# Who adds the pairs' probabilities at the end of attention: VectorE in GpSimd's place

## The reference

```
x = x + attn(layernorm(x))       # x: [2, 2048, 512] float32
x = x + ffn(layernorm(x))        # base linear layer, and 8 low-rank experts of which 2 are chosen

q, k, v = heads(x @ Wq.T), heads(x @ Wk.T), heads(x @ Wv.T)
q, k = rope(q), rope(k)
scores = einsum('bhqd,bhkd->bhqk', q, k) / sqrt(32), masked where k > q
attn = softmax(scores, axis=-1)
ctx = einsum('bhqk,bhkd->bhqd', attn, v)     # then @ Wo.T
```

## Time and profile before

| | |
|---|---|
| time, median of 3 runs | 1654.35 us (1653.99 to 1656.61) |
| profiled execution | 1654.52 us |
| its span | 1652.8 us |
| granted clock of TensorE, mean | 0.987 |
| busy: TensorE, VectorE, ScalarE, GpSimd | 97%, 69%, 46%, 54% of the span |
| GpSimd's additions L724 | 320 instructions, 619.3 us |

### The profile page before, as it was taken

How to read it: one execution, slowest core, us unless ns; L and a number is a source line. 1 busy time by engine, 2 the same in 40 slices (tenths; PEclk the granted TensorE clock), 3 DMA queues, 4 the chain that set the end, 5 groups by cost and what they waited for, 6 DMA issues and landing times. The chain is left out here.

```text
span 1652.8 us, 25687 instructions
## 1 busy us (share of the span) xinstructions
PE 1607.6 (97%) x9536; PEld 992.2 (60%) x9536; DVE 1142.6 (69%) x2253; ACT 764.2 (46%) x1539; POOL 886.4 (54%) x559
## 2 busy tenths in 40 slices
PE   6999999899999999999999999999999987999999
PEld 4888888555555555555555555545555435777776
DVE  5666666687777777777777777767777565665664
ACT  3222222145565556556556556556655663222221
POOL 2333324346677767667667767677767792112111
PEclk9999999689999999999999999999999999999999
DMA  5554784751134125115116107107103003222321
GB/s 191 197 196 172 228 292 153 197 122 33 28 86 95 27 62 118 27 41 133 34 22 153 27 18 163 27 8 173 27 8 109 8 33 102 77 77 77 113 91 51
DMA packets 112323, 157.01 MB, mean 95 GB/s; under 512 B 11600, under 2 KB 44880, under 8 KB 112208
## 3 DMA queue, kind: packets, MB, share of 16 engines
q1 hardware_dynamic: 102368, 136.10, 29.9%
q10 hardware_dynamic: 9840, 19.40, 3.3%
HBM read 96.23 MB, written 58.72 MB: 94 GB/s over the span
## 5 line engine op out<-in xcount | busy, mean ns | idle before, releaser
L857 ACT ACTIVATE a_probs<-a_st 128x512 f32<-128x512 f32 (+2 forms) x1244 | 579.0, 537 | 414.4 <-PE a_st L774 409.6
L724 POOL TENSOR_TENSOR a_pair<-a_probs 128x1024 f32<-128x1024 f32 (+2 forms) x320 | 619.3, 1956 | 196.6 <-ACT a_probs L857 189.3
L879 DVE TENSOR_REDUCE a_part<-a_mx 128x1 f32<-128x512 f32 (+2 forms) x864 | 550.9, 680 | 167.8 <-PE a_mx L758 129.2
L758 PE MATMUL a_mx<-a_k_stack,a_q_stack 96*128 96x512 f32 (+3 forms) x768 | 286.9, 399 | 1.2 <-DVE a_part L882 0.6
L774 PE MATMUL a_st<-a_q_stack,a_k_stack 98*128 98x512 f32 (+3 forms) x732 | 255.9, 369 | 0.0
L758 PEld LDWEIGHTS a_mx<-a_k_stack,a_q_stack 96*128 96x128 f32 x768 | 139.3, 189 | 173.2 <-DVE a_part L879 78.4
L882 DVE CUSTOM_DVE_ANT_0 a_mx<-a_mx,a_mask 128x384 f32<-128x384 f32 (+1 forms) x256 | 158.7, 631 | 79.9 <-PE a_mx L758 79.9
L258 POOL TENSOR_TENSOR p_rot<-p_mul 128x1024 f32<-128x1024 f32 x32 | 90.0, 2813 | 200.9 <-DVE p_mul L489 200.9
L758 PE MATMUL a_mx<-a_k_first,a_q_stack 96*128 96x512 f32 (+3 forms) x384 | 161.9, 445 | 2.6 <-DMA a_q_stack<-qk_scratch 1.8
L774 PEld LDWEIGHTS a_st<-a_q_stack,a_k_stack 98*128 98x128 f32 x732 | 138.4, 190 | 34.6 <-ACT a_probs L857 17.0
L1122 POOL TENSOR_TENSOR f_x<-f_x,f_bias 128x512 f32<-128x512 f32 x32 | 41.5, 1330 | 213.9 <-DVE f_xn L1334 213.9
(11 more groups left out here) (171 smaller groups left out, 2017.8 us busy)
## 6 DMA issues: line engine op xcount, KB each, us to landing
a_q_stack<-qk_scratch SPq DMA_DIRECT2D x72, 256.0 KB, 4.9
a_k_stack<-qk_scratch SPq DMA_DIRECT2D x72, 256.0 KB, 8.2
qk_scratch<-p_rot_hi SPq DMA_DIRECT2D x32, 512.0 KB, 3.1
qk_scratch<-p_rot_lo SPq DMA_DIRECT2D x32, 512.0 KB, 3.9
v_scratch<-p_v_st SPq DMA_DIRECT2D x32, 256.0 KB, 6.7
ctx_scratch<-a_ctx_st SPq DMA_DIRECT2D x32, 256.0 KB, 2.4
f_ctx<-ctx_scratch SPq DMA_DIRECT2D x8, 1024.0 KB, 8.8
f_x<-in_x SPq DMA_DIRECT2D x8, 1024.0 KB, 8.1
```

The costliest lines, as they stand in the source:

```text
L724: pool.tensor_tensor(pair[:, p % 2, h:h + 2, q0:TT], probs[:, s % RING, h:h + 2, q0:TT], probs[:, (s + 1) % RING, h:h + 2, q0:TT], ALU.add ...
L758: mm = pe.matmul(bank[:, i, :], queries[t][0:96, head, qi * P:(qi + 1) * P], keys[par][c][0:96, head, 0:width], start=(i == 0), stop=not m ...
L857: act.activation(probs[:, s % RING, h, q0:TT], score_bank(g, HG * s + h)[:, q0:TT], ACT.Exp, scale=SCORE_SCALE).then_inc(exp_done, 1)
L879: dve.tensor_reduce(found, bank.rearrange("p (h n) -> p h n", n=width), AX.X, ALU.max).then_inc(max_done, 1)
```

## The change

In the last group, from pair 10 on, the additions are no longer issued by GpSimd but by VectorE, in a function `add_pair` with the same instructions, waits and semaphores. VectorE does this at the head of pair p, ahead of its split for the next stage and ahead of the transposes of a unit that ended with the pair before. Where the pair lies on the diagonal, VectorE waits for GpSimd's masking. GpSimd keeps the masking and the divisions. All other groups stay as they are.

```
+NO_ITEMS = min(p for p in range(NPAIR) if items_before(p, False) >= NITEM)
...
-        no_items = min(p for p in range(NPAIR) if items_before(p, False) >= NITEM)
-        SIX_FROM = HG * (2 * no_items + 2)
+        SIX_FROM = HG * (2 * NO_ITEMS + 2)
...
-                    pool.wait_ge(pair_done, pairs(g, p - 2))
-                    for h in range(0, HG, 2):
-                        pool.wait_ge(exp_done, exps(g, s + 1, h + 1))
-                        pool.tensor_tensor(pair[:, p % 2, h:h + 2, q0:TT], probs[:, s % RING, h:h + 2, q0:TT],
-                                           probs[:, (s + 1) % RING, h:h + 2, q0:TT], ALU.add).then_inc(pair_added, 1)
+                    if not (g == GROUPS - 1 and p >= NO_ITEMS):
+                        pool.wait_ge(pair_done, pairs(g, p - 2))
+                        for h in range(0, HG, 2):
+                            pool.wait_ge(exp_done, exps(g, s + 1, h + 1))
+                            pool.tensor_tensor(pair[:, p % 2, h:h + 2, q0:TT], probs[:, s % RING, h:h + 2, q0:TT],
+                                               probs[:, (s + 1) % RING, h:h + 2, q0:TT], ALU.add).then_inc(pair_added, 1)
...
+            def add_pair(g, p):
+
+                s = 2 * p
+                t, j = STEPS[s]
+                q0 = max(0, j + 1 - t * SUB) * P
+                if j >= t * SUB:
+                    dve.wait_ge(masked, diagonal_steps(g, s + 1))
+                dve.wait_ge(pair_done, pairs(g, p - 2))
+                for h in range(0, HG, 2):
+                    dve.wait_ge(exp_done, exps(g, s + 1, h + 1))
+                    dve.tensor_tensor(pair[:, p % 2, h:h + 2, q0:TT], probs[:, s % RING, h:h + 2, q0:TT],
+                                      probs[:, (s + 1) % RING, h:h + 2, q0:TT], ALU.add).then_inc(pair_added, 1)
+
             def group(g, first, last):
                 for p in range(NPAIR):
+                    if last and p >= NO_ITEMS:
+                        add_pair(g, p)
                     if last and SPLIT_FROM <= p <= SPLIT_FROM + KT:
                         split_early(p - SPLIT_FROM)
```

## The result

The changed kernel takes 1646.47 us in the median (1644.32 to 1646.91, 6 runs), the kernel before beside it 1655.48 us (1653.32 to 1658.80, 6 runs). The forecast gain was 7.1 us, counted from an execution of 1654.52 us.

A forecast was written before the change was run, and what follows sets the result against it. GpSimd's additions were taken to bound pairs 13 to 17 of the last head group. TensorE waits of 7.37 us go and 0.3 come back, a gain of 7.1 us: from 1654.52 to 1647.4 us, range 1645.0 to 1650.8.

The forecast's parts named there:

- GpSimd is the bound of pairs 13 to 17 by its additions: Last head group: two additions beside the split take GpSimd 5.74 us a pair, 0.4 us over TensorE's work.
- VectorE's price of 1.22, 0.95 and 0.42 us: Cost of one moved addition on VectorE for 128x1024, 128x768 and 128x256.
- The slow rival: VectorE's queue becomes the bound, a 128x1024 addition costing 5.5 us: 1711 us; chance 4%.
- The forecast's threshold of 2.5 us: Cost of an addition on VectorE from about which the change was expected to make the kernel slower.
- VectorE keeps up, by 3.7 us: In full pairs VectorE needs 3.8 of 5.33 us, and its addition is there 3.7 us before TensorE's sums.
- That rival's 5.6 us for a pair: ScalarE takes over if its exponentials take 0.63 us: 1.4 us less gain, 1648.8 us; chance 6%.
- 5.33 us of TensorE's work in a full pair: TensorE's own time for a full pair, read from pair 15, in which nothing seemed to wait.
- Pair 10: First moved pair: a TensorE wait of 0.39 us goes.
- Pair 17: Its 6.44 us, partly at half clock after a stall, fall to 5.33 at full clock: 1.11 us gained.
- The tail: Pairs 18 and 19: TensorE's waits of 0.57 and 0.85 us go, 1.42 us gained.
- 0.3 us come back at the end: Pairs 18 and 19: maskings and additions around the large split cost between nothing and 0.5 us, taken as 0.3.
- The transposes behind the additions in pair 12 are hidden: Pair 12: VectorE's transpose of the previous unit's sums ends before TensorE's sums are due, with 1.7 us left.

The follow-up runs named there:

- e1: Kernel before, additions still on GpSimd, with VectorE's split in pairs 13 to 17 cut to eight columns of each block: 1648.19 us, ratio 0.9956.
- e10: Changed kernel, with GpSimd also making two additions of 128x1024 between spare tiles in pairs 12 to 17: 1657.24 us, ratio 1.0016 to the kernel before.
- e4: Changed kernel, with every moved addition done twice on VectorE, once into a spare tile: 1657.23 us, ratio 1.0017 to the kernel before.
- e3: Kernel before, with only the additions of diagonal pairs 10, 11, 18 and 19 moved to VectorE: 1653.81 us, ratio 0.9986.
- e9: Changed kernel, with the split of pairs 13 to 17 cut to eight columns of each block: 1646.92 us, ratio 0.9955 to the kernel before.
- e8: Changed kernel, but in pair 12 VectorE turns the unit's sums before it makes the pair's additions: 1645.98 us, a single run.
- e5: Changed kernel, with VectorE's second addition in pairs 12 to 17 waiting for TensorE's head 0 scores of the next step: 1651.05 us, ratio 0.9981.

## Why the prediction was right, and where it was off

The mechanism held, the time was forecast to 0.9 us, and part of that closeness is luck: the gain was 9.0 us by the medians and 9.2 by the stretch, not 7.1, and the kernel before ran at 1655.48 us in its six runs, 1.0 us above the 1654.52 from which the forecast counted. Term by term:

- *GpSimd is the bound of pairs 13 to 17 by its additions*: right. That the split's slowing was most of it the prediction had in its numbers (4.8 against 5.74 us) but not in its account: e1 gets 6.3 us by taking the split away alone.
- *VectorE's price of 1.22, 0.95 and 0.42 us*: right, but for the one addition beside the division (2.14 us). The slow rival asked for 5.5 us; with GpSimd busy the mean is 2.07 (e10). The forecast's threshold of 2.5 us was too high: e4 spends 2.4 us for each addition and is 1.9 us slower by the stretch, for the transposes in pair 12 and the large split in pair 17 share the queue. Where the threshold lies below 2.4 us no run shows.
- *VectorE keeps up, by 3.7 us*: right, by 3.05 us in pairs 14 to 16 and 1.95 in pair 13. ScalarE didn't take over either; it was busy 4.1 to 4.2 us of 5.12. That rival's 5.6 us for a pair doesn't follow from 8 x 0.63, which is 5.0.
- *5.33 us of TensorE's work in a full pair*: wrong, 5.12. It was read from a pair that showed no stall and held a hidden wait of 0.2 us. This is the mis-sized term: the gains of pairs 12 to 17 were 6.92 us, not 5.56.
- *Pair 10*: 0.31 us, not 0.39. The 0.39 is the idle time of the weight loads, which overstates a loss; the matmuls' own was 0.12.
- *Pair 17*: 1.56 us, not 1.11, partly for the 0.2 us above. Its own work is 4.88 us; the next step's scores are 384 wide. The half clock went as forecast; e1, with no stall ahead of pair 17, has none either (granted clock 1.00), and e3, with the stall, has the 6.44 us again, at 0.74.
- *The tail*: 1.95 us, not 1.42, which counted only the two named waits of TensorE. Of the other 0.53 us, 0.19 lie ahead of pair 18's `sums` and 0.31 between those of 18 and 19. Both times TensorE started 0.06 us behind GpSimd's addition, so they look like more of the same wait; no run separates them.
- *0.3 us come back at the end*: nothing did. The first masking of pair 18 does wait behind the large split: it took 2.22 us instead of 0.63, 1.6 us more, where 1.7 us of VectorE's subtraction were left when it started. The Trainium skill, SBUF — State Buffer, section "Who interferes with whom", has the later one blocked for the whole of the other's instruction; the trace agrees. But the additions of pair 18 ended 0.5 us ahead of their `sums` and those of pair 19 0.16 us, and e9, without the split, is no shorter.
- *The transposes behind the additions in pair 12 are hidden*: right, and the other order costs 0.78 us (e8).
- *The next tile's load goes out at about 1353.3 and stays ahead of the store*: right, 1353.35 against 1361.94.
- *What a stall costs*: in e4, e5 and e10 each long wait of TensorE, of 2.5 to 4 us, was followed by a stretch at a mean granted clock of 0.57 to 0.68. The prediction had this for pair 17 alone; its slow rivals were priced without it.

## What to carry to other kernels

When two engines both look late or slow in the same stretch, compare each one's instruction there with the same shape elsewhere: here an addition at 2.87 rather than 2.36 us and a subtraction at 2.77 rather than 0.69 said more than the busy shares, and taking away either partner freed the other. Read an engine's own pace from a stretch in which its input was early by the producer's record, not from one that merely shows no idle time; look at the weight loads' idle time as well, against that of a pair that surely had its input early, and remember that a part of it costs nothing (0.60 us here). Work moved to an engine's queue should go ahead of its long, unhurried items, and what a moved step lets start (here a division) may collide with it.

## What the runs showed of the hardware

- A two-input VectorE instruction in SBUF and a GpSimd instruction there delay each other, in both directions: VectorE's subtraction of 128x512 went from 0.69 to 2.77 us, GpSimd's addition from 2.36 to 2.87 us and its two maskings from 1.27 to 2.81 us. The split's cast, which has one input, was delayed too, 0.42 to 2.60 us. The maskings had never met this before the change: all 128 took 0.63 us.
- A stall of TensorE of 0.1 to 0.2 us leaves no idle time in its row, only in that of its weight loads: 0.84 to 0.91 us where 0.30 is usual and 0.60 still cost nothing.
- The start of pair 9's `sums` in the profiled executions, which has the same code ahead of it in nearly all of these kernels, lay between 1311.95 and 1316.05 us. Two things move it. Attention's first product of scores into `a_st` began between 330.19 and 333.09 us; of the changed kernel's 1.7 us against the kernel before, 1.15 were there already. From that product to pair 9's `sums` it took 981.0 to 985.5 us, the longer the lower the mean granted clock, 0.996 to 0.990; and what is missing from 1.00 lies ahead of 420 us in all of these executions. The columns as in the earlier trace rows, for the changed kernel (1314.18) and e3 (1316.05):

```profile
330.00:420.00 90.00, 86.87 (x495) 45.95 (x496) 72.79 (x153) 43.81 (x91) 47.65 (x33) 0.93 0.31 71
```

```profile
330.00:420.00 90.00, 87.06 (x480) 47.00 (x483) 69.90 (x142) 43.51 (x91) 46.54 (x31) 0.89 0.32 71
```

The clock at a stage's opening differs from one execution to the next, and with it the time, here by up to 4.5 us; that is why the stretch, not the time, was the measure here.
